# A relational layer in one pass made into two, and clears added to or taken from three streams of gathers and scatters, in a four layer graph network

## The reference: what is computed

```python
x = x + L0(h)   # three rounds of x' = x' + sigmoid(gat(x')), one head; self loops
x = x + L1(h)   # relational: relu(norm * segment_sum(msg, dst) + h @ loop)
x = x + L2(h)   # gat with 8 heads of 16; self loops
x = x + L3(h)   # edge conditioned messages, divided by their count, then a linear layer
```

```python
c_e = coefficients[rel_type]                    # 4 numbers an edge
msg = c_e[:, 0] * (h @ basis[0])[src] + ... + c_e[:, 3] * (h @ basis[3])[src]
out = relu(segment_sum(msg, dst) * norm + h @ loop_weight)
```

## Time and profile before

| what | us |
|---|---|
| median of the runs | 3954.9 |
| profiled execution | 3923.35 |
| its span, first to last instruction | 3921.4 |
| PE busy | 2263.7 (58%) |
| DVE busy | 2282.0 (58%) |
| POOL busy | 2157.8 (55%) |
| ACT busy | 1610.7 (41%) |
| DMA moved | 380.48 MB, mean 97 GB/s |

### The profile page before, as it was taken

One profiled execution on the slowest core, in us unless ns is written; L12 is line 12 of the kernel. 1 busy time (PEld: TensorE's weight loads), 2 busy tenths in 40 slices (PEclk: granted clock), 3 DMA queues, 4 the chain that ended last, 5 costly groups with the idle time before them and its releaser, 6 DMA issues. The chain is left out here.

```text
span 3921.4 us, 53964 instructions
## 1 busy us (share of the span) xinstructions
PE 2263.7 (58%) x12833; PEld 1777.4 (45%) x12833; DVE 2282.0 (58%) x8009; ACT 1610.7 (41%) x3565; POOL 2157.8 (55%) x2121
## 2 busy tenths in 40 slices
PE   1035899999898565465565567754526443344333
PEld 1023676676677554364464444434425332233222
DVE  4154999999898785334345378866575333333233
ACT  0005999999997573223323322324411222122100
POOL 3618765575564332581185255546500588888755
PEclk9998999999999786577577588887756666666665
DMA  2140122332231454651663733333304333333253
GB/s 64 27 181 20 44 90 87 100 103 87 87 92 39 133 157 116 161 139 42 186 174 87 203 95 99 87 98 81 90 16 118 109 74 64 75 74 65 51 145 117
DMA packets 569029, 380.48 MB, mean 97 GB/s; under 512 B 51389, under 2 KB 511942, under 8 KB 568386
## 3 DMA queue, kind: packets, MB, share of 16 engines
q1 hardware_dynamic: 510050, 329.99, 28.7%
q0 software_dynamic: 56000, 46.29, 6.4%
q10 hardware_dynamic: 2720, 1.23, 0.2%
HBM read 249.08 MB, written 153.32 MB: 103 GB/s over the span
## 5 line engine op out<-in xcount | busy, mean ns | idle before, releaser
L1309 POOL DMA_INDIRECT p_a<-t_d,k_map_ix x300 | 309.1, 1030 | 291.3 <-DMA p_a<-t_d 241.1
L807 POOL TENSOR_TENSOR a_rs<-a_ve,w_neg_half 128x16 f32<-128x16 f32 x113 | 330.1, 2922 | 241.7 <-DVE a_ve L743 227.7
L833 ACT ACTIVATE a_nr<-a_xb,a_nm,a_rs 128x128 f32<-128x128 f32 x882 | 369.9, 487 | 26.1 <-POOL a_nm L809 26.1
L2064 POOL DMA_INDIRECT e_a<-t_d,e_ix x200 | 210.4, 1052 | 277.1 <-DMA e_a<-t_s 219.2
L895 PE MATMUL a_ps<-w_ident,a_nr 128*128 128x128 f32 x1568 | 245.6, 280 | 128.8 <-DVE a_xb L754 47.3
L903 PE MATMUL a_ps<-a_ht,w_aug 128*128 128x512 f32 x588 | 312.7, 616 | 2.4 <-DVE a_ht L710 2.4
L895 PEld LDWEIGHTS a_ps<-w_ident,a_nr 128*128 128x128 f32 x1568 | 179.9, 143 | 277.0 <-issue 244.5
L1431 PE MATMUL p_pm<-w_aug,p_ht 128*128 128x130 f32 (+1 forms) x1600 | 277.1, 343 | 7.6 <-ACT p_ht L1392 3.8
L710 DVE TENSOR_TENSOR a_ht<-a_ps,a_ht 128x512 f32<-128x512 f32 x294 | 201.5, 686 | 134.7 <-ACT a_ps L848 111.0
L1431 PEld LDWEIGHTS p_pm<-w_aug,p_ht 128*128 128x128 f32 x1600 | 261.4, 250 | 21.4 <-ACT p_ht L1392 11.9
L1789 PE MATMUL c_pq<-layer_src,c_sel 128*128 (+1 forms) x800 | 194.3, 420 | 124.7 <-ACT c_sel L1760 72.2
(11 more groups left out here) (358 smaller groups left out, 6449.0 us busy)
## 6 DMA issues: line engine op xcount, KB each, us to landing
t_s<-p_a SPq DMA_DIRECT2D x100, 256.0 KB
c_a<-t_d SPq DMA_DIRECT2D x100, 256.0 KB
t_d<-c_a SPq DMA_DIRECT2D x100, 256.0 KB
a_xa<-in_x SPq DMA_DIRECT2D x98, 256.0 KB
out<-a_xb SPq DMA_DIRECT2D x98, 256.0 KB, 2.0
p_a<-t_s SPq DMA_DIRECT2D x75, 256.0 KB
p_a<-t_d SPq DMA_DIRECT2D x75, 256.0 KB
t_acc<-q_zt SPq DMA_DIRECT2D x3, 2171.5 KB
```

The source lines that it names most:

```text
L807: nc.gpsimd.tensor_tensor(RS[:, z, :], VE[:, z, :], w["neg_half"][:, None, 0:J].to_broadcast([P, LNS, J]), ALU.pow).then_inc(s_rstd.sem, 1)
L833: last = nc.scalar.activation(NR[k][:, T.at(NORM[k], 2), cols(j)], normed_rows(T, k)[:, cols(j)], ACT.Identity, bias=NM[:, T.at(1, SHORT), ...
L1309: eng.indirect_dma_start(out=A[:, g, SRC, j, :], out_offset=None, in_=t[f"d{r}"], in_offset=bass.IndirectOffsetOnAxis(ap=k["map_ix"][:, b ...
L2064: eng.indirect_dma_start(out=A[:, g, side, j, :], out_offset=None, in_=t[f"d{r}"], in_offset=bass.IndirectOffsetOnAxis(ap=IX[:, g, what, j ...
```

## The change

All edits in one:
- In `keys` POOL waits and clears a tile after each of its 100 scatters, as `project` does. DVE takes the in-degree of each edge's target from the row numbers of the first and the last edge of its run (two scans and their carries over tiles) and its inverse root by three Newton steps; `coef` becomes the coefficients times that root. `hold_ix` and `prev_col` go.
- `project` clears no more where it takes norms, which of the projections with gathers is r = 4; r = 1 and 2 keep the clears.
- `relate` becomes pass one with a ring of 7, written out, no clears. It writes `s4` as before, and puts the mix with the loop message into `keep`, in SBUF. `aggregate` with the new kind "relate" is pass two, not weighted, with the relu in its last add; it writes `d4` for every row.
- In every `aggregate` SP sends four of the eight end DMAs, before its stream of loads, ACT the other four; the two row DMAs go ahead of the last copy of partial sums, on a semaphore of their own; the sigmoid's lag is 2.
- `attend` of layer 2 is called with `whole=True`: two spreads are not made.
- `edge_messages` loads the target rows with a plain DMA of SP in place of the gather by `hold_ix`.
- `edge_outputs` is written out with a ring of 8, takes its indices without a copy, and POOL waits and clears after each of its 100 scatters.

```diff
@@ keys, gpsimd
                                        in_=ID[:, c:c + 1], in_offset=None, bounds_check=NODES * WORDS - 1, oob_is_err=False).then_inc(s_map1, 16)
+                if c:
+                    eng.wait_ge(s_idle, c)
+                nc.gpsimd.memset(IDLE[:, :], 0.0).then_inc(s_idle, 1)
@@ keys, vector
+            done(v.tensor_scalar(FX[:, :], FF[:, :], -1.0, 1.0, ALU.mult, ALU.add))
+            done(v.tensor_tensor(HV[:, :], IRF[:, :], FF[:, :], ALU.mult))
+            done(v.tensor_tensor_scan(FO[:, :], FX[:, :], HV[:, :], 0.0, ALU.mult, ALU.add))
...
+            done(v.scalar_tensor_tensor(deg, HL[:, :], 1.0, FO[:, :], ALU.add, ALU.subtract))
+            done(v.tensor_scalar(half, deg, -0.5, None, ALU.mult))
+            done(v.tensor_scalar(root.bitcast(I32), deg.bitcast(I32), -0.5, 1597463007.0, ALU.mult, ALU.add))
+            for step in range(3):
+                done(v.tensor_tensor(HV[:, :], root, root, ALU.mult))
+                done(v.tensor_tensor(HV[:, :], HV[:, :], half, ALU.mult))
+                last = v.scalar_tensor_tensor(root, HV[:, :], 1.5, root, ALU.add, ALU.mult)
...
-                v.tensor_scalar(k["coef"][:, bass.ds(b * J, J), :], PC[:, 0:J * BASES].rearrange("p (j b) -> p j b", j=J), 1.0, None, ALU.mult).then_inc(s_loop, 1)
+                v.tensor_tensor(k["coef"][:, bass.ds(b * J, J), :], PC[:, 0:J * BASES].rearrange("p (j b) -> p j b", j=J),
+                                NORM[:, bass.ds(b * J, J), :].to_broadcast([P, J, BASES]), ALU.mult).then_inc(s_loop, 1)
@@ project, gpsimd
-                        if b * J + j:
-                            eng.wait_ge(s_idle, b * J + j)
-                        nc.gpsimd.memset(IDLE[:, :], 0.0).then_inc(s_idle, 1)
+                        if not norm:
+                            if b * J + j:
+                                eng.wait_ge(s_idle, b * J + j)
+                            nc.gpsimd.memset(IDLE[:, :], 0.0).then_inc(s_idle, 1)
@@ aggregate
+            eng.wait_ge(s_part, BANKS)
+            end_sums(eng, range(J // 2))
             stream(eng, (load, 0), *([(store_sel, 2)] if first else []), (store, 3))
...
+                    v.scalar_tensor_tensor(A[:, g, :, :], PS[g][:, :, :], 0.0, A[:, g, :, :], ALU.max, ALU.add).then_inc(s_next, 1)
...
+                if n == BANKS - 1:
+                    if weighted:
+                        eng.wait_ge(s_ms, BLOCKS)
+                    for s, row in enumerate((0, P - 1)):
+                        eng.dma_start(ENDT[:, 2 + s:3 + s, :], keep["src"][row:row + 1, :, 0:C]).then_inc(s_rows_in, 16)
...
-            stream(eng, (widen, 0), *([(squash, 1)] if sigmoid else []))
+            stream(eng, (widen, 0), *([(squash, 2)] if sigmoid else []))
@@ relate, gpsimd and vector
+            for b in range(BLOCKS):
+                g = b % RING
+                eng.wait_ge(s_load[g], uses(b) * 32)
+                for j in range(J):
+                    m = b * J + j
+                    if b:
+                        eng.wait_ge(s_over[j], 16 * b)
+                    eng.indirect_dma_start(out=A[:, g, SRC, j, :], out_offset=None, in_=t[f"d{r}"],
...
+            def residual(b):
+                g = b % RING
+                eng.wait_ge(s_mm, b * 2 + 1)
+                there(eng, b)
                 v.scalar_tensor_tensor(A[:, g, SRC, :, :], PM[SRC][:, :, :], 0.0, A[:, g, SRC, :, :], ALU.max, ALU.add).then_inc(s_next, 1)
+            def mix(b):
+                for base, j in ((base, j) for half in range(0, J, 2) for base in range(1, BASES) for j in (half, half + 1)):
+                    m = b * J + j
+                    if base == 1:
+                        eng.wait_ge(s_base, m + 1)
+                    else:
+                        eng.wait_ge(s_mix, mixed(b, base - 1, j))
+                    v.scalar_tensor_tensor(keep["src"][:, m, :], PB[j][:, base, :], k["coef"][:, m, base:base + 1], keep["src"][:, m, :],
+                                           ALU.mult, ALU.add).then_inc(s_mix, 1)
+            for n in range(BLOCKS + 3):
+                if n <= BLOCKS:
+                    if n < BLOCKS:
+                        there(eng, n)
+                    mo.turn(eng, lambda m: A[:, n % RING, m // J, m % J, :], n, BLOCKS - 1)
+                if 0 <= n - 3:
+                    residual(n - 3)
+                    mix(n - 3)
@@ relate, scalar
+            for n in range(BLOCKS + 1):
+                if n < BLOCKS:
+                    apply(n)
+                if n:
+                    loop(n - 1)
+                    base(n - 1)
+                if n < BLOCKS:
+                    copy(n)
@@ edge_messages
+                wait(eng, s_out[g], (b // GE) * (16 * J))
+                carry_waits(eng, w)
+                eng.dma_start(A[:, g, DST, :, :], block_rows(t[f"d{r}"], b)).then_inc(s_dst[g], 16)
...
                     gather(b, g, MAP, SRC, j, s_over[g])
-                    gather(b, g, HOLD, DST, j, s_hold[g])
@@ edge_outputs, gpsimd
+            for b in range(BLOCKS):
+                g = b % RING
+                eng.wait_ge(s_out_in, b + 1)
                 for j in range(J):
+                    m = b * J + j
+                    eng.indirect_dma_start(out=out, out_offset=bass.IndirectOffsetOnAxis(ap=k["out_s_ix"][:, m:m + 1], axis=0),
                                            in_=SZ[:, g, j, :], in_offset=None,
                                            bounds_check=N - 1, oob_is_err=False).then_inc(s_out[g], 16)
+                    if m:
+                        eng.wait_ge(s_idle, m)
+                    nc.gpsimd.memset(IDLE[:, :], 0.0).then_inc(s_idle, 1)
@@ layer 1 and layer 2
+        keep = held(nc, ctx, "layer1", C)
+        relate(nc, w, k, t, 3, keep)
+        aggregate(nc, w, k, t, 3, "relate", 1, keep, None, None, False, False)
...
-        attend(nc, w, k, 4, HEADS, keep, wm, ws, False)
+        attend(nc, w, k, 4, HEADS, keep, wm, ws, True)
```

More of the change, by code:

```diff
@@ new lines, in _ @@
+            deg, half, root = (DEG[:, n, :] for n in range(3))
+            done(v.scalar_tensor_tensor(deg, HL[:, :], 1.0, FO[:, :], ALU.add, ALU.subtract))
[5 more added lines that the diff above has]
+                last = v.scalar_tensor_tensor(root, HV[:, :], 1.5, root, ALU.add, ALU.mult)
+                if step < 2:
+                    done(last)
@@ L1824, in relate @@
-        PM = [ps(f"pm{n}", [P, J, C]) for n in range(2)]
-        PB = [ps(f"pb{n}", [P, BASES, C]) for n in range(2)]
-        PS = [ps(f"ps{n}", [P, 512]) for n in range(2)]
-        s_tp, s_ht, s_mm, s_loop, s_next, s_next_dst, s_basis, s_mix, s_sel, s_pe, s_sum, s_zero, s_deg, s_pow, s_mean, s_num, s_coef = (
-            sem(n) for n in "tp ht mm loop next next_dst basis mix sel pe sum zero deg pow mean num coef".split())
-        s_kb = [sem(f"kb{g}") for g in range(GE)]
-        s_out = [sem(f"out{g}") for g in range(GE)]
@@ L1831, in relate @@
-        block = ctx.enter_context(nc.Block())
+        mo = Moments(nc, ctx, pre + "mo", w, SHORT, 2 * J)
+        PT = [ps(f"pt{s}", [P, J, C]) for s in range(2)]
+        PM = [ps(f"pm{s}", [P, J, C]) for s in range(2)]
+        PB = [ps(f"pb{j}", [P, BASES, C]) for j in range(J)]
+        s_tp, s_ht, s_mm, s_next, s_loop, s_basis, s_base, s_mix = (sem(n) for n in "tp ht mm next loop basis base mix".split())
+        s_normed = [sem(f"normed_{side}") for side in ("src", "dst")]
+        s_load, s_out = ([sem(f"{n}{g}") for g in range(RING)] for n in ("load", "out"))
@@ L1999, in edge_messages @@
+            for n in range(BLOCKS):
+                turn(n)
+                product(n)
 def edge_messages(nc, w, k, t, r, out):
     M = C + 1
-    MAP, HOLD, ACC, OUT = range(4)
+    MAP, ACC, OUT = range(3)
     with phase(nc) as ctx:
@@ L2251, in edge_outputs @@
+        s_cnt, s_tp, s_s, s_mm, s_up, s_out_in, s_idle = (sem(n) for n in "cnt tp s mm up out_in idle".split())
+        s_load, s_out = ([sem(f"{n}{g}") for g in range(RING)] for n in ("load", "out"))
         block = ctx.enter_context(nc.Block())
-        before = lambda b, g: b - (1 if g == 0 else 2)
+        uses = lambda b: b // RING + 1
         @block.sync
         def _(eng):
-            def load(b, g):
-                wait(eng, s_out[g], (b // GE) * (16 * J))
-                carry_waits(eng, w)
+            for b in range(BLOCKS):
+                g = b % RING
+                if b >= RING:
+                    eng.wait_ge(s_out[g], (uses(b) - 1) * (16 * J))
```

418 lines of the change are left out of this document (175 added, 243 removed).

## The result

The changed kernel takes 3688.88 us (median of four runs, 3685.27 to 3690.87) against 3953.85 of the kernel before in the same job (3951.69 to 3956.05): a ratio of 0.933, 95% interval 0.9313 to 0.9345. The forecast was 3684, and faster. Its profiled execution took 3690.87 (span 3688.9). So each phase is set against both. The span also holds the set-up, the three short attends of layer 0 and `rows_found`, which are not listed and stay within 0.3 us each. A phase is taken from its first instruction in the trace to the first one of the next phase.

The account below looks back on a forecast made before the run. Barrier-separated phases, each with its own bound, so the end is their sum. Terms -54, -49, -20, -7, -16, -120 and -5 make -271: 3652 profiled, with 31.6 for the median 3684 us; range 3645 to 3775.

Parts of the forecast that it names:

- Keys, -54: Keys: with clears DVE runs its 25 rounds beside the scatters, POOL is the end; 218 against 272, -54 us.
- 2 for the landing and 3.5 for the barrier: End of keys: us added after POOL's last step at 212, making 218.
- The first rival: Keys and outputs: clears release nothing, +10 and +20 in place of -54 and -5; 3773 us, chance 0.12.
- Relational layer, -49: Relational layer in two passes: 225 + 4 + 105 = 334 against 384 us, DVE setting pass one's turn; bounds -70, -5.
- Aggregates, -20: Four other aggregates: split end DMAs and earlier row DMAs save 5 us each, -20; bounds -24 and +8.
- meets no wait on the path: Aggregates: the sigmoid's lag of two costs 0 us; bounds -4 and +4.
- Projection r=4, -7: Layer 2's projection without clears: four gathers shrink, 0.56 us per pair of turns, 12 pairs, -7; bounds -15 and +30.
- the third rival's mild form: Pass one and projection r=4: two or three stalls from uncleared gathers, +30 to +45, at 3720 us; chance 0.05.
- The sign that the forecast named for it: Pass one or projection r=4: a DVE PSUM reader idle over 5 us, an old DMA named, would prove the forecast wrong.
- the third rival: Pass one and projection r=4: uncleared gathers stall DVE 14.8 us at a time, slower than before, 3958 and more; chance 0.03.
- Attend, messages, outputs: Two spreads dropped, -16.4 us; held gathers dropped, messages' turn 21.1, -120; outputs' cleared scatters without pauses, -5.

Follow-up runs that it names:

- the swapped kernel: The changed kernel with clears reversed: none in keys, outputs and projections r=1, 2; clears in pass one and projection r=4; 3762 us, ratio 0.954.
- the second profile of before: The kernel before, unchanged, profiled once more: 3953.0 us, span 3951.0, where its first profile had 3923.35, span 3921.4.

## Why the prediction was right, and where its steps were not

**Keys, -54; measured -45.** The mechanism is as forecast: clears free DVE, POOL is the end. The next phase's first scatter is at 227.75, 10 behind the forecast. POOL's row is 4 of it: it starts at 64.7 (63.7 forecast) and its period is 1.52 over all, not 1.49. The term most mis-sized is the end: 2 for the landing and 3.5 for the barrier became 11.3, as POOL's drain of 8.22 us was left out. It stood in the trace before, at 188.4, hidden by DVE's rounds. The first rival (clears release nothing) is out by the 256.8 of the swapped kernel. It said that no row shows what holds L447: the trace shows that it is PE's signal that comes late, and nothing shows why.

**Relational layer, -49; measured -57 to -60.** The turn was taken as 8.1 and is 7.0 to 7.2, as interleaved multiply-adds take 0.27 and not 0.35. PE's busy time is 6.6 a turn, for 6 or less forecast, and still below DVE's. Against this the first residual comes 47 us after the start and not 30; in the kernels with clears it comes after 33 to 34, so 13 of the 17 are the late signals. Pass two took 109 for 105.

**Aggregates, -20; measured -6 to 0.** The step that failed is that the sigmoid's lag of two "meets no wait on the path": it costs 6.6 in round 0, outside the bound of 4. And of the 5 each, 0.8 are lost in r=4 because the two row DMAs stand ahead of ACT's last copy. What else kept r=2 at 124.1, for 121.6 and 123.4 before, is open.

**Projection r=4, -7; measured +5 to +11.** This step failed. It is the third rival's mild form: beside gathers without clears, signals reach ACT and DVE 1 to 3 us late in the burst. The sign that the forecast named for it, a PSUM reader of DVE idle for over 5 us with an old DMA named, did not come; ACT and small DVE instructions waited, with no releaser named. How much of the +5 to +11 is theirs is not settled, as the same code took 240.2 to 246.6. What spoke against it in the forecast, that L1911 of the one-pass layer idles for only 10.6 us, was true and no evidence: that layer gathers four at a time between POOL's own arithmetic (one signal is late there, by 1.5 us), and the projection opens with a burst of 28, as the third rival itself said.

**Attend, messages, outputs.** -16.4, -120 and -5 were measured as -17, -125 to -129 and -3 to -10. The messages' turn is 20.5 for 21.1. In outputs the scatters run without stalls, 147.3 from first start to last end for the forecast's 148.5, but the clears give nothing by it: without them the phase took 168.9 and 167.5. So the gain there is not theirs; the ring of 8 and the indices without a copy are what is left of the edit, not tested apart.

**The sum.** The forecast of 3684 is the median of before less 271; the measured difference of medians is 265. Against the second profile of before it is 262, against the first only 232. Within the sum steps that were too hopeful (keys 9, aggregates 14 to 20, r=4 12 to 18) stand against steps that were too careful (relational layer 8 to 11, messages 5 to 9, outputs up to 5). So the total is nearer than its terms, and in that it was lucky. And it holds where the stalls are: keys took 250 with them and 178.7 without, and in the jobs without them before has 100 us less to lose.

## What to carry to other kernels

Take a long burst of GpSimd's indirect DMAs as something that can make the signals of other engines late and slow SP, and read waits with an absurd or no releaser as its mark; a clear that put 0.2 us more between two removed it here, in the jobs that had it. What it costs is the burst's length, and in a job without the stalls that cost stands alone. So it belongs where others must work beside the burst (keys, projections, pass one) and not where POOL is the bound anyway (outputs). When POOL becomes the last engine of a phase, add its drain to the sum. Where a gather only repeats what a better table could hold, as the held rows did, dropping it is worth its full POOL time: 100 gathers, 127 us. And profile the base twice before terms of ten us are set against it.

## What the runs showed of the hardware

- In keys, indirect DMAs of POOL follow each other at 1.28 us in the plain step (0.98 and 0.30); a clear of one column between two does not change that, one of 256 columns makes it 1.47.
- Beside such a stream semaphores are counted up long after the instruction that does it has ended: PE's for DVE by up to 18.6 us in keys before, PE's for ACT by up to 17.7 in a projection, DVE's for DVE itself by up to 3.2 in r=4. A register move of SP takes 1002 ns at the median in place of 29.
- It was so in three jobs, where the kernel before took 3937 to 3954 us; in the other two it took 3850 and 3840. The code of its keys took 249.4 and 250.7 in two of the three and 178.7 in one of the two.
- A drain of POOL takes 8.22 us at the end of keys and of outputs, before and after. With what lies around it, 11.3 us pass from POOL's last clear of keys to the next phase's first scatter; in outputs the last scatter of the earlier trace rows begins at 3910.0 and the span ends at 3921.4.
